# Experts' batch 0 prepared on ScalarE and behind the last scan, first loads issued ahead of two barriers, last heads joined on VectorE

## What is computed

```python
h = _layernorm(x) * (1 + ca) + sa
x = x + ga * _L0_attn_ref(h, ...)     # out = (a1 - lam * a2) @ v, normed per head, @ Wo
x = x + gb * _L0_ffn_ref(...)
# layer 1, the scan: per state n, hs = dA * hs + dB, y = sum_n C_n * hs
x = x + ga * _L1_attn_ref(h, ...)
# layer 1, the experts
h = _layernorm(x) * (1 + cb) + sb
aff = h @ centroids.T
_, idx = top_k(aff + expert_biases, 8)
w = sigmoid(aff[idx]); w = w / (sum(w) + 1e-08)
x = x + gb * (shared(h) + sum_e cw[t, e] * (silu(h @ W_up[e]) @ W_down[e]))
```

## Time and profile before

| | |
|---|---|
| median of 3 runs | 1686.43 us (1686.24 to 1691.65) |
| the profiled execution | 1685.61 us, its span 1683.9 us |
| TensorE, VectorE busy | 77%, 73% of the span |
| ScalarE, GpSimd busy | 62%, 55% |
| granted TensorE clock, mean | 0.893 |

### The profile page before, as it was taken

The page is one execution under the profiler, slowest core; times in us unless marked ns, Lnnn a source line. Parts: engine busy times, 40 slices in busy tenths (PEclk is TensorE's granted clock), DMA queues, the critical chain, the costliest instruction groups (busy, mean ns, idle before and its releaser), DMA issues. The chain is left out here.

```text
span 1683.9 us, 29244 instructions
## 1 busy us (share of the span) xinstructions
PE 1297.4 (77%) x8526; PEld 578.4 (34%) x8589; DVE 1234.9 (73%) x2038; ACT 1044.1 (62%) x1641; POOL 921.8 (55%) x833
## 2 busy tenths in 40 slices
PE   4588888787878788874567557776756999999998
PEld 3133333333333333332234322222212444444444
DVE  4667767767776867785478679999997776666763
ACT  2167767576757766764465446656533878787776
POOL 3033525243442534343488537877764778777777
PEclk8589999899999999988777777888779999999999
DMA  5231313222221313110000057776755977777785
GB/s 135 76 106 47 109 37 95 59 78 67 77 77 57 90 56 95 40 30 2 0 1 0 2 165 268 264 260 206 241 194 149 199 179 193 183 184 190 184 187 136
DMA packets 123691, 198.75 MB, mean 118 GB/s; under 512 B 24604, under 2 KB 60088, under 8 KB 123576
## 3 DMA queue, kind: packets, MB, share of 16 engines
q1 hardware_dynamic: 122136, 195.08, 40.9%
q10 hardware_dynamic: 1440, 2.10, 0.4%
HBM read 167.76 MB, written 28.84 MB: 117 GB/s over the span
## 5 line engine op out<-in xcount | busy, mean ns | idle before, releaser
L960 DVE TENSOR_REDUCE bmax<-p1b 128x4 f32<-128x512 f32 x640 | 410.8, 685 | 136.4 <-PE p1b L705 131.3
L643 ACT ACTIVATE pT<-p2b 128x512 f32<-128x512 f32 x640 | 349.1, 602 | 190.2 <-PE p2b L757 189.1
L2095 POOL TENSOR_TENSOR hid_l<-e_hid,w_experts 128x1024 f16<-128x1024 f32 (+1 forms) x136 | 281.2, 2083 | 100.8 <-ACT w_experts L2230 99.8
L594 POOL CAST nsp<-qneg 128x16 bf16<-128x16 f32 x64 | 12.6, 196 | 438.7 <-DVE qneg L971 438.7
L2329 DVE TENSOR_TENSOR e_hid<-ub,share 128x1024 f32<-128x1024 f32 x128 | 155.8, 1222 | 118.6 <-ACT ub L2241 106.4
L1798 PE MATMUL yb<-ch,ident 128*128 128x512 f32 x256 | 143.9, 697 | 65.4 <-POOL ch L1765 65.4
L772 PE MATMUL ob<-pT,vs 128*32 128x512 f32 (+3 forms) x2048 | 190.4, 460 | 1.9 <-POOL pT L603 1.2
L757 PE MATMUL p2b<-qs,ks 50*128 50x512 bf16 (+3 forms) x1024 | 131.3, 315 | 56.6 <-ACT pT L643 44.8
L2230 ACT ACTIVATE w_experts<-e_hid 128x1024 f16<-128x1024 f32 (+1 forms) x136 | 139.4, 1026 | 38.6 <-DVE e_hid L2329 38.5
L2241 ACT ACTIVATE ub<-ub 128x1024 f32<-128x1024 f32 (+1 forms) x136 | 134.0, 985 | 37.7 <-PE ub L2146 35.9
L603 POOL TENSOR_SCALAR_AFFINE_SELECT pT<-pT 128x1280 f32<-128x1280 f32 (+2 forms) x192 | 145.0, 787 | 11.5 <-ACT pT L643 11.5
(11 more groups left out here) (282 smaller groups left out, 2489.5 us busy)
## 6 DMA issues: line engine op xcount, KB each, us to landing
share<-shares SPq DMA_DIRECT2D x256, 256.0 KB, 4.3
brow<-bc_rows SPq DMA_DIRECT2D x64, 512.0 KB, 4.2
crow<-bc_rows SPq DMA_DIRECT2D x64, 512.0 KB, 5.1
q_stacks<-parts SPq DMA_DIRECT2D x96, 128.0 KB
k_stacks<-parts SPq DMA_DIRECT2D x96, 128.0 KB
qs<-q_stacks SPq DMA_DIRECT2D x128, 96.0 KB, 2.3
ks<-k_stacks SPq DMA_DIRECT2D x128, 96.0 KB, 2.4
qs<-nparts SPq DMA_DIRECT2D x128, 4.0 KB
```

What stands on the lines that cost most here:

```text
L643: act.activation(pT[:, g2 % 2, stored(w), :], p2b[bank_of(g2, w)][:, :], ACT.Exp, scale=SCALE).then_inc(exp_done, 1)
L960: dve.tensor_reduce(to, bank, AX, ALU.max).then_inc(first_read, 1)
L2095: pool.tensor_tensor(flat(hid_l[:, rounded(p), 0:n, :]), flat(hid[:, place(p), 0:n, :]), flat(hid_h[:, rounded(p), 0:n, :]), ALU.subtract) ...
```

## The change

It has five parts.

1. Attention, last batch only: the two products and the sum that join the maps of each head run on VectorE behind its reciprocals, no longer on GpSimd.
2. FFN: SyncE, between the two stores of rows, loads B and C of batch 0's first two pairs into the scan's rings, and behind the second store the third and fourth C. The rings are allocated earlier for this, and three FFN tiles use memory that is free by then (`gate_a0`, `wraw`).
3. Scan, batches 6 and 7: the statistics of the experts' batch 0 go from round 6, m = 3, to round 7, m = 0, with an added instruction for the negated means; normalizing is two ScalarE steps of four instructions (`centre` at n = 7, `spread` at n = 9); transposing goes to m = 5, the copies to n = 13, routing to m = 7, and bias, maxima and strike behind the last scan, all in the drain's order ahead of the choice. GpSimd's split of h goes from behind its pass 5 to behind its pass 6. The gates are scaled between the last residual and batch 1's statistics.
4. Scan, drain round: SyncE, behind the store of the shares, waits for it and issues the eight loads of the experts' first four steps; the ring for them lies in `k.w`, whose place for the rounded values moves up.
5. Experts: SyncE leaves those loads out in round 0. In the loop it waits for the saved shares ahead of each step's loads.

```diff
@@ attention, VectorE
                         dve.reciprocal(rc[:, :, :, :].rearrange("p c h j -> p c (h j)"), oT[:, (r + 1) % 2, :, :, VD]).then_inc(rc_ready, 1)
+                        if isinstance(r, int) and r == B:
+                            ...
+                            dve.wait_ge(rc_ready, pb + 1)
+                            dve.wait_ge(merged_ready, pb + 1)
+                            for j, to in enumerate((og, o2)):
+                                dve.tensor_tensor(to[:, :, :], o[:, :, j, :], rcv[:, :, j].unsqueeze(2).broadcast_to(full), ALU.mult).then_inc(og_parts, 1)
+                            dve.wait_ge(og_parts, 2)
+                            dve.tensor_tensor(og[:, :, :], og[:, :, :], o2[:, :, :], ALU.add).then_inc(og_ready, 1)
@@ ffn, SyncE
-            for b in range(2):
-                front.store_rows(sp, b)
+            front.store_rows(sp, 0)
+            sp.wait_ge(front.bc_saved, 16)
+            for m in range(2):
+                front.load_b(sp, 0, m)
+                front.load_c(sp, 0, m)
+            front.store_rows(sp, 1)
+            for m in range(2, C_RING):
+                front.load_c(sp, 0, m)
             sp.wait_ge(x_ready, B + 1)
             sp.wait_ge(front.bc_saved, 2 * 16)
@@ ExpertEntry
+    def load_share(self, sp, b, p):
+        if not isinstance(b, int) or p == 0:
+            sp.wait_ge(self.shares_saved, (b + 1) * 16)
+        rows = self.shares_dram[b, 4 * p:4 * p + 4, :].rearrange("(t a) s -> a t s", a=2)
+        for a in range(2):
+            sp.dma_start(self.share[a * EF:(a + 1) * EF, p % SHARES, :, :],
+                         rows[a, :, :].partition_broadcast(EF)).then_inc(self.share_loaded[p % SHARES], 16)
-    def norm(self, dve):
+    def minus_means(self, dve):
+        dve.tensor_scalar(self.stat[:, :, 1], self.stat[:, :, 0], -1.0, None, ALU.mult).then_inc(self.stat_ready, 1)
+    def centre(self, act):
+        act.wait_ge(self.stat_ready, 1)
         for c in range(TILES):
-            ins = dve.tensor_scalar(self.xn[:, c, :], self.k.x[:, c, :], self.stat[:, c, 0:1], self.rstd[:, c:c + 1], ALU.subtract, ALU.mult)
+            ins = act.activation(self.xn[:, c, :], self.k.x[:, c, :], ACT.Identity, bias=self.stat[:, c, 1:2])
+        ins.then_inc(self.centred, 1)
+    def spread(self, act):
+        act.wait_ge(self.centred, 1)
+        for c in range(TILES):
+            ins = act.activation(self.xn[:, c, :], self.xn[:, c, :], ACT.Copy, scale=self.rstd[:, c:c + 1])
         ins.then_inc(self.xn_ready, 1)
@@ scan, SyncE
                     entry.store_shares(sp)
+                    for p in range(SHARES):
+                        entry.load_share(sp, 0, p)
                     return
 ...
             rounds(sp, step)
             sp.wait_ge(x_ready, B + 1)
-            sp.wait_ge(entry.shares_saved, 16)
@@ scan, GpSimd
-                    if r == B - 1 and m == PAIRS - 3:
+                    if r == B - 1 and m == PAIRS - 2:
                         entry.split_h(pool)
@@ scan, TensorE
-                    if r == B - 1 and m == 1:
+                    if r == B - 1 and m == 5:
                         entry.turn(pe, front.preb)
-                    if r == B - 1 and m == 4:
+                    if r == B - 1 and m == PAIRS - 1:
                         entry.route(pe, front.preb)
@@ scan, ScalarE
                     if r == B - 1 and n == 7:
+                        entry.centre(act)
+                    if r == B - 1 and n == 9:
+                        entry.spread(act)
+                    if r == B - 1 and n == 13:
                         entry.copy_h(act, front.preb)
@@ scan, VectorE
                     residual()
+                    entry.gates(dve)
                     dve.wait_ge(x_ready, 2 + 1)
                     entry.batch_stats(dve, 1)
 ...
-                    if r == B - 2 and m == 3:
+                    if r == B - 1 and m == 0:
                         dve.wait_ge(x_ready, 1 + 1)
                         entry.batch_stats(dve, 0)
-                        entry.gates(dve)
-                    if r == B - 1 and m == 0:
-                        entry.norm(dve)
-                    if r == B - 1 and m == 5:
+                        entry.minus_means(dve)
+                    if r == B - 1 and m == PAIRS - 1:
                         entry.bias(dve, front.preb)
-                    if r == B - 1 and m == 6:
                         entry.largest(dve)
-                    if r == B - 1 and m == PAIRS - 1:
                         entry.strike(dve)
```

More of the change, by code:

```diff
@@ L585, in slot @@
                 full = [P, TILES * H, VD]
+                alone = isinstance(r, int) and r == B
                 if on(1):
@@ L604, in slot @@
                                            pattern=[[0, n], [1, P]], channel_multiplier=-1).then_inc(masked, 1)
-                if post and g == 4:
+                if post and g == 4 and not alone:
                     pool.wait_ge(rc_ready, pb + 1)
@@ L609, in slot @@
                     pool.tensor_tensor(o2[:, :, :], o[:, :, 1, :], rcv[:, :, 1].unsqueeze(2).broadcast_to(full), ALU.mult).then_inc(pool_own, 1)
-                if post and g == 5:
+                if post and g == 5 and not alone:
                     pool.wait_ge(pool_own, pb * 2 + 2)
@@ L1082, in __init__ @@
         self.dt = sb("dt", [P, 2, S])
+        self.brow, self.crow = sb("brow", [P, 2, 2, S]), sb("crow", [P, C_RING, 2, S])
+        self.b_loaded, self.c_loaded = [sem(f"b_loaded{n}") for n in range(2)], [sem(f"c_loaded{n}") for n in range(C_RING)]
         self.preb, self.pre2, self.dtxb = ps("s_preb"), ps("s_pre2"), ps("dtxb")
@@ L1103, in store_rows, with load_pair, load_b, load_c @@
         sp.dma_start(self.bc_dram[b, :, :], self.bc[:, :]).then_inc(self.bc_saved, 16)
+    def load_pair(self, sp, b, m, tile, first, loaded):
+        slot = m % len(loaded)
+        sp.dma_start(tile[:, slot, :, :].rearrange("p j s -> p (j s)"),
+                     self.bc_dram[b, first + 2 * m:first + 2 * m + 2, :].rearrange("j s -> (j s)").partition_broadcast(P)).then_inc(loaded[slot], 16)
+    def load_b(self, sp, b, m):
+        self.load_pair(sp, b, m, self.brow, 0, self.b_loaded)
+    def load_c(self, sp, b, m):
+        self.load_pair(sp, b, m, self.crow, N, self.c_loaded)
     def turn(self, pe, b):
@@ L1326, in step @@
                         pe.wait_ge(hid_ready, b * FT + j + 1)
-                        pe.matmul(upb[j % 2][:, :], w1[:, j * P:(j + 1) * P], hT[:, :], start=True, stop=True).then_inc(up_done, 1)
+                        pe.matmul(upb[j % 2][:, :], w1[:, j * P:(j + 1) * P], hT, start=True, stop=True).then_inc(up_done, 1)
                 if down:
@@ L1520, in __init__ @@
         self.hTl = k.w2[:, :, :].rearrange("p j n -> p (j n)").bitcast(FP16).rearrange("p (a s) -> p a s", a=2)
+        spent = k.w[:, :, :].rearrange("p a c -> p (a c)")
+        self.share = spent[:, 0:SHARES * 2 * S].rearrange("p (n j s) -> p n j s", n=SHARES, j=2)
+        self.rounded = spent[:, SHARES * 2 * S:].bitcast(FP16)
+        self.share_loaded = [sem(f"share_loaded{n}") for n in range(SHARES)]
         self.centT = sb("centT", [P, E])
@@ L2000, in experts @@
         yb, sideb = ps("e_yb"), ps("e_sideb")
-        share_loaded = [sem(f"share_loaded{s}") for s in range(SHARES)]
         shares_saved = entry.shares_saved
@@ L2020, in rounded, with rounded_half @@
             return p % (ROUNDED - 1) if p < PAIRS else ROUNDED - 1
+        def rounded_half(p, n, slots):
+            at = (rounded(p) * 2 + n) * S
+            return entry.rounded[:, at:at + slots * S]
         def pair_set(p):
@@ L2060, in step @@
                 if main:
-                    sp.wait_ge(shares_saved, (r + 1) * 16)
                     for p in range(PAIRS):
+                        if not post and p < SHARES:
+                            continue
                         before = p - SHARES if p >= SHARES else p - SHARES - 1
-                        if p >= SHARES or post:
-                            sp.wait_ge(hid_ready, r * STEPS + before + 1 + RING)
-                        rows = shares_dram[r, 4 * p:4 * p + 4, :].rearrange("(t a) s -> a t s", a=2)
-                        for a in range(2):
-                            sp.dma_start(share[a * EF:(a + 1) * EF, p % SHARES, :, :],
-                                         rows[a, :, :].partition_broadcast(EF)).then_inc(share_loaded[p % SHARES], 16)
+                        sp.wait_ge(hid_ready, r * STEPS + before + 1 + RING)
+                        entry.load_share(sp, r, p)
                         if post and p == TURN_AT + SHARES + 1:
```

38 lines of the change are left out of this document (17 added, 21 removed).

## The result

The changed kernel takes 1679.39 us (median of 11 runs, 1672.47 to 1683.99), the kernel before 1688.42 us (11 runs, 1686.23 to 1692.53): ratio 0.994, 95% interval 0.9922 to 0.9957. The medians lie 9.0 us apart; the gain is clear of the spread, though under 1%. The profiled execution took 1675.72 us with a span of 1674.0, 9.9 us less than the 1683.9 before.

What follows compares the result with a forecast made beforehand. VectorE was taken to bound the scan, TensorE the experts, and the barrier's chain the seams. Terms -2.6 - 3.95 - 6.8 + 4.15 - 0.3 = -9.5 us gave 1676.1 profiled and 1677.0 us as median; range 1672 to 1682.

Steps and rivals of the forecast that it cites:

- Attention: End of attention: three passes moved from GpSimd to VectorE take about 3.75 us instead of 6.35, 2.6 us less.
- First scan: Scan entry: early rows let the first scan start 3.95 us earlier, with ScalarE's decays then coming last.
- rival 3: Scan entry: early rows gain nothing because something else is as late; 3.95 us more, 1680.9; chance 0.07.
- Batch 6: Scans of batch 6: the statistics' 8.35 us between fourth and fifth scan all goes.
- what is late next: Batch 6: seventh scan needs GpSimd's fourth pass, ending 1234.51; scan due 1234.69, so it just fits, 0.2 us to spare.
- Batch 7: Scans of batch 7: moved statistics bring the second scan 2.0 us later; gaps before the last two scans lose 0.45 us.
- Rival 2: Batch 7: statistics again fall beside GpSimd's passes and cost 8.35 us; 4.2 us more, 1681.2; chance 0.13.
- Behind the last scan: After the last scan: added VectorE work stays hidden; choice ends near T + 4.8, ahead of the residual at T + 6.0.
- The added wait: Barrier before the experts: SyncE's eight load issues open it 4.15 us later; early shares buy 0.3 us.
- Rival 1: Barrier before the experts: issuing the eight loads does not hold it; 4.15 us less, 1672.8; chance 0.07.
- rival 4: Barrier before the experts waits for early shares to land, not their issue; 6.3 us behind forecast's SyncE, 1683.3; chance 0.05.
- rival 5: Experts' first batch: TensorE's clock stays low after longer idling; 34.5 us more, 1711; chance 0.03.

Runs made afterwards that it cites:

- the two kernels that move the split: Against the changed kernel, GpSimd's last split of weights goes from batch 6 to batch 7, behind pass 0 or pass 2; executed once: 1680.0 and 1673.2 us.
- the one that brings the pause back: Against the changed kernel, the statistics alone go back to batch 6, behind scan 3; executed once, 1689.9 us.
- the line of 11.5, 11.7, 13.0 and 15.6: Changed kernel with none, one, two or all four shares loaded ahead of the barrier: first expert product, in us after the last scan's end T.
- the two queues: Against the changed kernel, ScalarE issues four of the eight early loads, SyncE the other four; 1678.89 us, ratio 0.9941 to the kernel before; start T + 13.3.

## Why the prediction came out

1677.0 us was forecast, 1679.39 is the median, and 1675.7 the profiled execution, for which 1676.1 was worked out. Most of the 2.4 us between the forecast and the median lies in the base, not in a step: the forecast started from a median of three runs, 1686.43, where eleven give 1688.42, 2.0 more. The change itself was put at 9.5 us; the medians lie 9.0 apart. That the profiled execution was met within 0.4 us is in part luck: the steps came out 0.5 us short, and stretches that no step names were 0.9 us shorter.

- **Attention**: -2.6 forecast, -2.75 measured (undoing it alone: 2.75). Right.
- **First scan**: -3.95 forecast and measured; undone alone 3.52, with a faster landing. ScalarE came last, as said, and rival 3 falls.
- **Batch 6**: 8.35 us were to go, 7.48 did. The seventh scan fits, as said; the step that failed is "what is late next". I stopped at GpSimd's fourth pass and did not follow the backlog on to its split of weights, which had been early only because the statistics held the scans. That term was 0.87 us too large: the split held VectorE's product for 1.20 us, and 0.32 us came back at the first logarithm step, as the two kernels that move the split and the one that brings the pause back show.
- **Batch 7**: +2.0 forecast, +1.89 measured; the two gaps before the last scans -0.47 instead of -0.45. Rival 2 falls: the statistics cost 3.93 us, since GpSimd's only pass there (1244.42, 2.35 us) ends just as the first small arithmetic begins (1246.74). With a split put there it was 6.6.
- **Behind the last scan**: the choice ends at T + 4.7 (forecast 4.8) and the residual starts at T + 6.0, as before. The comparison took 0.42 us. It began 0.01 us after GpSimd's last pass was over, so the trace agrees with the rule that the prediction quoted from the Trainium skill, SBUF — State Buffer, section "SBUF: two separate sides": the 1.37 us were a wait.
- **The added wait**: +4.15 forecast, +4.2 measured, +4.1 when undone; what it bought was put at 0.3. The experts' first batch is 0.4 us shorter than in the kernel before (its 17th multiplication comes at 46.9 us, before at 47.3), but undoing the early loads alone loses 0.1; no run shows what gave the other 0.3. Rival 1 falls with the line of 11.5, 11.7, 13.0 and 15.6, rival 4 with the two queues (13.3 for the same eight loads). Rival 4's lateness was also added up wrongly: from 1300.74 to 1307.2 it is 6.5 us, not 6.3.
- **Clock**: rival 5 falls. Busy time in three stretches from 1283.5 us on, columns as in the earlier trace rows:

```profile
1283.50:1288.00 4.50, 0.00 (x0) 0.00 (x0) 0.00 (x0) 0.00 (x0) 0.00 (x0) 0.50 1.01 234
1288.00:1293.00 5.00, 4.70 (x14) 1.76 (x15) 0.00 (x0) 1.88 (x2) 0.00 (x0) 0.60 1.00 210
1293.00:1298.00 5.00, 3.37 (x18) 1.59 (x17) 4.49 (x7) 4.38 (x6) 2.10 (x1) 1.00 0.29 92
```

TensorE was idle for 9.2 us, nearly twice as long as in the kernel with the shares behind the barrier (5.1), started at the lower level (0.50 is 1.2 of 2.4 GHz) and was back at 1.00 by 1293, no later after its start than in the earlier trace rows. The first of these lines also shows the early shares being moved (234 GB/s) while every engine waits at the barrier.

The steps sum to -2.75 - 3.95 - 7.48 + 1.89 - 0.47 + 4.2 - 0.4 = -9.0. The spans differ by 9.9. The remaining 0.9 is spread in pieces of 0.1 to 0.4 us over stretches with the same instructions (up to the reciprocal, the FFN, batches 0 to 5 of the scan, the experts behind their first batch), which vary by more than that among these profiles.

## What to carry to other kernels

Loads moved ahead of a barrier are free only while the issuing queue has slack: count the issues (0.66 us each here) against the engine that reaches the barrier last, and move just as many as that engine covers. Ask as well what the early loads buy: here four early shares cost 4.1 us at the start and saved 0.1 behind it. Small VectorE chains cost what GpSimd does beside them; put them where its pass has just ended, not where VectorE seems free. When a pause goes, follow the engine that used the pause to catch up as far as its last job in the round.

## What was not expected of the hardware

- A TENSOR_SCALAR with one input of 128x4 elements was held for 2.87 us by GpSimd's split, and in the kernel before one took 1.05 us at the place of the earlier trace rows. The rule quoted from the Trainium skill, SBUF — State Buffer, section "SBUF: two separate sides", names two SBUF inputs, and beside them VectorE's faster modes that use both ports. Whether this instruction runs in such a mode no trace here shows; the hold itself is measured.
- The hold goes both ways. In batch 6 of the changed kernel VectorE's first logarithm step (L1234, both inputs in SBUF) took 1.48 us from 1230.94, until 0.6 us after the end of GpSimd's pass (1231.86); the pass that GpSimd began at 1231.83 took 2.80 us instead of 2.35, as if it had waited for that step. In the kernel before, GpSimd's split met the same step so and took 3.30 us (from 1247.76; the step ended at 1248.36) instead of 2.86. The four steps behind it, with one input in PSUM, ran beside this pass at 0.73 us each.
- Attention, the same instructions in every profile but for its end, took up to its last reciprocal 785.5 us in the changed kernel and 798.3 in the kernel with the statistics back. The granted clock was 0.91 and 0.89 in the stretch up to 785 us. That is wider than the whole change and the reason why its parts had to be read in the trace. What sets it stayed open.
